# Splitting the overflow rows' sums on POOL into two half-precision parts for the scatter on TensorE

## The reference

```python
# layer 0
mask = (adj > 0.0)
h = relu(h[:, :, None, :] @ W1a + (h[:, :, None, :] - h[:, None, :, :]) @ W1b + b1)   # per edge j, k
hm = einsum('bjkh,bjk->bjh', h, mask)        # sum over the neighbours k of node j
x = x + hm @ W2 + deg[..., None] * b2
# layer 1
x = x + (adj @ relu(layernorm(x))) @ W3.T
```

## Time and profile before

| | us |
|---|---|
| median of 3 runs | 905.98 (905.89 to 906.07) |
| profiled execution | 904.65 |
| its span, first to last instruction | 902.6 |
| granted TensorE clock, mean | 0.983 |

### The profile page before, as it was taken

How to read it: one execution, slowest core, us unless ns; L and a number is a source line. 1 busy time by engine, 2 the same in 40 slices (tenths; PEclk the granted TensorE clock), 3 DMA queues, 4 the chain that set the end, 5 groups by cost and what they waited for, 6 DMA issues and landing times.

```text
span 902.6 us, 27715 instructions
## 1 busy us (share of the span) xinstructions
PE 862.0 (96%) x8626; PEld 771.7 (86%) x8627; DVE 866.4 (96%) x3032; ACT 775.9 (86%) x1728; POOL 698.8 (77%) x1548
## 2 busy tenths in 40 slices
PE   3879999999999999999999999999999999999996
PEld 1448999989998989999999999998999899989995
DVE  6989999999999999999999999999999999999993
ACT  4858989898989898989889898988898889898983
POOL 0857787888888888888887878787878788888874
PEclk9789999999999999999999999999999999999997
DMA  9700000000000000000000000000000000000000
GB/s 341 279 1 5 20 11 20 16 20 17 19 17 20 11 20 17 20 17 20 15 14 16 20 17 19 17 18 18 12 20 16 20 16 20 16 20 11 7 8 16
DMA packets 26549, 27.58 MB, mean 31 GB/s; under 512 B 3360, under 2 KB 24352, under 8 KB 25376
## 3 DMA queue, kind: packets, MB, share of 16 engines
q1 hardware_dynamic: 25488, 25.37, 8.3%
q10 hardware_dynamic: 912, 0.39, 0.2%
HBM read 21.56 MB, written 4.19 MB: 29 GB/s over the span
## 4 chain that ended last, share of the span: by engine, by line
PE 69%; DVE 19%; issue 5%; ACT 3%; POOL 2%; DMA 1%; SPq 0%; ACTq 0%; POOLq 0%; DVEq 0%
PE ring L378 36%; DVE acc L763 12%; PE ring L406 6%; PE post L465 4%; PE post L464 4%; PE prep L435 4%; PE post L470 4%; PE prep L445 3%; PE prep L442 2%; DVE onehot_space L749 2%; PE prep L441 2%; ACT ring L530 1%; POOL rstd L915 1%; DMA x_all<-x_nbf_dram 1%; DVE onehot_row L804 1%
## 5 line engine op out<-in xcount | busy, mean ns | idle before, releaser
L763 DVE SCALAR_TENSOR_TENSOR acc<-ring,acc 128x384 f32<-128x384 f32 x896 | 489.0, 546 | 1.1 <-PE ring L378 0.2
L530 ACT COPY ring<-P 128x768 f32<-128x768 f32 x512 | 403.3, 811 | 16.3 <-DVE acc L763 6.9
L378 PE MATMUL ring<-PQ,onehot_space 128*128 128x192 f16 x4096 | 404.0, 247 | 7.2 <-ACT ring L530 3.3
L378 PEld LDWEIGHTS ring<-PQ,onehot_space 128*128 128x128 f16 x4096 | 338.2, 100 | 31.7 <-ACT ring L530 19.2
L864 POOL TENSOR_TENSOR relu_row<-relu_row 128x192 f32<-128x192 f32 x256 | 151.8, 593 | 101.1 <-ACT relu_row L562 91.1
L749 DVE TENSOR_SCALAR onehot_space<-mask_all 128x512 f16<-128x512 f16 x512 | 155.2, 305 | 0.0
L583 ACT ACTIVATE h<-x_all,shift,rstd 128x64 f32<-128x64 f32 x128 | 56.3, 440 | 83.6 <-POOL shift L883 83.6
L851 POOL TENSOR_SCALAR start<-P,spare 128x192 f32<-128x192 f32 x128 | 121.1, 946 | 5.9 <-ACT P L576 5.1
L464 PE MATMUL post<-consts,acc 128*128 128x128 f32 x512 | 98.5, 274 | 1.5 <-POOL relu_row L864 1.5
L465 PE MATMUL post<-ownerT,relu_row 128*128 128x128 f32 x512 | 99.0, 275 | 0.0
L406 PE MATMUL ring<-PQ,owner 128*128 128x384 f16 (+1 forms) x512 | 94.1, 306 | 0.0
(11 more groups left out here) (129 smaller groups left out, 1616.0 us busy)
## 6 DMA issues: line engine op xcount, KB each, us to landing
onehot_space<-adj_kbj_dram SPq DMA_DIRECT2D x8, 1024.0 KB, 17.1
adj_again<-adj_kbj_dram SPq DMA_DIRECT2D x128, 64.0 KB, 1.9
x_all<-x_nbf_dram SPq DMA_DIRECT2D x8, 512.0 KB, 17.8
out_dram<-x_all SPq DMA_DIRECT2D x32, 128.0 KB, 1.7
consts<-consts_dram SPq DMA_DIRECT2D x1, 192.0 KB, 2.6
scratch<-w1a_dram ACTq DMA_DIRECT2D x2, 48.0 KB, 4.3
scratch<-w1b_dram ACTq DMA_DIRECT2D x2, 48.0 KB, 6.7
scratch<-b_dram ACTq DMA_DIRECT2D x1, 96.0 KB, 10.0
```

Of the source, the lines that this page charges most:

```text
L378: last = nc.tensor.matmul(to, hot(s), parts[:, part, H:2 * H], start=False, stop=(part == 1), skip_group_check=True)
L530: return nc.scalar.copy(slots[to], src.unsqueeze(1).unsqueeze(1).broadcast_to([N, BANKS, PER_BANK, H]))
L763: return nc.vector.scalar_tensor_tensor(sums, slots[to][:, bank_], 0.0, start[:, :, :] if first else sums, ALU.max, ALU.subtract if first ...
```

## The change

The overflow sums are no longer handed over in fp32. POOL adds the first two slots as before, adds the third and writes the result rounded to half precision (`high`), subtracts that from the sum of the first two, and adds the third slot to the difference, written in half precision (`low`). The four operations are chained by semaphores. The new tensor `hm_row` holds both parts, its last columns cleared once. Before writing it POOL also waits for a count of `transposed` that covers the matmuls of the graph before. `ownerT` becomes half precision. TensorE scatters the two parts with two half-precision matmuls in place of one fp32 matmul for each half of the hidden columns.

```diff
--- before.py
+++ after.py
@@ -139,12 +139,13 @@
         onehot_row = sb("onehot_row", [N, SLOTS, N], F16)
         from_first = sb("from_first", [N, N], F16)
         owner = sb("owner", [N, 2, N], F16)
-        ownerT = sb("ownerT", [N, 2, N])
+        ownerT = sb("ownerT", [N, 2, N], F16)
         code_row = sb("code_row", [N, N], F16)
         start = sb("start", [N, PER_BANK, H])
         acc_space = sb("acc", [N, 2, ROW + N - H2])
         acc = acc_space[:, :, 0:ROW].rearrange("p g (s h) -> p g s h", h=H)
         relu_row = sb("relu_row", [N, ROW_SLOTS, H])
+        hm_row = sb("hm_row", [N, 2, 2 * N], F16)
 
         sums_T = sb("sums_T", [N, 3, N])
         hmT, aggT = sums_T[:, 0:2, :], sums_T[:, 2, :]
@@ -227,6 +228,8 @@
         loop_half_summed = sem("loop_half_summed")
         loop_summed = sem("loop_summed")
         half_row_ready = sem("half_row_ready")
+        hm_high_ready = sem("hm_high_ready")
+        hm_rest_ready = sem("hm_rest_ready")
         hm_row_ready = sem("hm_row_ready")
         sums_T_ready = sem("sums_T_ready")
         bias_ready = sem("bias_ready")
@@ -457,12 +460,13 @@
                                 pe.wait_ge(loop_summed, load(nc.tensor, 0, b - 1) + load(nc.tensor, 1, b - 1) + 1)
                             pe.wait_ge(summed, b * REGULAR)
                             pe.wait_ge(hm_row_ready, b)
-                            hm_row = relu_row[:, :, :].rearrange("p s h -> p (s h)")
                             for k in range(2):
                                 for s in range(PER_BANK):
                                     hm = acc_space[:, (u + 1) % 2, s * H + k * N:s * H + (k + 1) * N]
                                     nc.tensor.matmul(sums_T_ps[:, k, :], hm, ident, start=(s == 0), stop=False, is_transpose=True)
-                                last = nc.tensor.matmul(sums_T_ps[:, k, :], hm_row[:, k * N:(k + 1) * N], ownerT[:, (u + 1) % 2, :], start=False, stop=True)
+                                for part in range(2):
+                                    last = nc.tensor.matmul(sums_T_ps[:, k, :], hm_row[:, part, k * N:(k + 1) * N], ownerT[:, (u + 1) % 2, :],
+                                                            start=False, stop=(part == 1))
                         if exists(b - 3):
                             pe.wait_ge(h2_ready, b - 2)
                             at, times = mixed_at(b, u, t)
@@ -635,6 +639,7 @@
             nc.vector.memset(w2b[H2:N, :], 0.0)
             nc.vector.memset(w3t[F:N, :], 0.0)
             nc.vector.memset(acc_space[:, :, ROW:], 0.0)
+            nc.vector.memset(hm_row[:, :, H:], 0.0)
             nc.vector.memset(start[:, :, :], 0.0).then_inc(loop_summed, 1)
             dve.wait_ge(consts_in, 16)
             nc.vector.tensor_tensor(upto, before, ident, ALU.add)
@@ -859,13 +864,17 @@
                 if exists(b - 1):
 
                     pool.wait_ge(relu_row_ready, b)
-                    sums = relu_row[:, 0, :]
-                    for s in range(1, ROW_SLOTS):
-                        last = nc.gpsimd.tensor_tensor(sums, sums, relu_row[:, s, :], ALU.add)
-                        if s < ROW_SLOTS - 1:
-                            last.then_inc(half_row_ready, 1)
-                            pool.wait_ge(half_row_ready, (b - 1) * (ROW_SLOTS - 2) + s)
-                    last.then_inc(hm_row_ready, 1)
+                    half, rest, third = (relu_row[:, s, :] for s in range(ROW_SLOTS))
+                    high, low = hm_row[:, 0, 0:H], hm_row[:, 1, 0:H]
+                    nc.gpsimd.tensor_tensor(half, half, rest, ALU.add).then_inc(half_row_ready, 1)
+                    if exists(b - 2):
+                        pool.wait_ge(transposed, b + 2)
+                    pool.wait_ge(half_row_ready, b)
+                    nc.gpsimd.tensor_tensor(high, half, third, ALU.add).then_inc(hm_high_ready, 1)
+                    wait_apart(pool, hm_high_ready, b)
+                    nc.gpsimd.tensor_tensor(rest, half, high, ALU.subtract).then_inc(hm_rest_ready, 1)
+                    wait_apart(pool, hm_rest_ready, b)
+                    nc.gpsimd.tensor_tensor(low, rest, third, ALU.add).then_inc(hm_row_ready, 1)
                 if exists(b - 3):
 
                     k = (u + 1) % 2
```

## The result

The changed kernel takes 1050.62 us (median of 4 runs, 1050.46 to 1051.89) against 905.98 us before. One of the four runs of the kernel before was a slow one, 2185.14 us, and is left out of its median. The ratio is 1.160 (95% interval 1.1577 to 1.1622). The forecast was 1052. The profiled execution took 1050.59 us, its span is 1048.6 us.

The account below looks back on a forecast made before the run. The prediction took the POOL-ScalarE loop (6.38 us per graph) as the bound. 121 periods growing from 6.48 to 7.63 us give 139 us, the ends 6.7 and 0.3: +146 on 904.65, plus 1.3: 1052 us, range 1022 to 1084.

Parts of the forecast that it names:

- The path: POOL's added work ahead of the second norm lengthens the POOL-ScalarE loop in full, +1.33 us per graph.
- the bound I had set: Each new POOL operation was bounded by two rows of the same width, 551 and 593 ns.
- The hop with two waits: Between POOL's first two adds, a second, long fulfilled wait adds 0 to 0.07 us, taken as 0.035.
- L880's operation: Power in POOL's second norm, 0.73 us mid-run and 0.57 at the end; half the difference taken, -0.08 us.
- 0.09 of slack: In ScalarE's part of the loop, a seed's wait for VectorE's last sum: 6.47 - 0.09 = 6.38 us.
- TensorE's saving: Half-precision scatter matmuls on TensorE save 0.2 us per graph, worth nothing while the loop binds.
- VectorE's own work: VectorE's work per graph without waiting in the kernel before, put at 6.3 us or more.
- the three bounds: Per graph in the kernel before: the loop 6.38 us, VectorE about 6.3, TensorE 6.14.
- faster: Rival, 3%: the fp32 scatter on TensorE bounds and POOL's additions vanish in its idle time, 884 us.
- POOL's order alone: Rival, 7%: ScalarE's wait for the shift does not close the loop; period 7.14 us, time 990 us.
- Longer operations beside VectorE: Rival, 6%: VectorE's work lengthens POOL's new operations, +0.48 us per graph, period 8.1 us, time 1110 us.
- TensorE's clock: Rival, 2%: TensorE's clock falls to half, 11.8 us per graph, about 1580 us.

Follow-up runs that it names:

- e5: Kernel before with one more POOL add of 192 fp32 columns per graph, last in POOL's step, outside the loop: 907.8 us, ratio 1.0005.
- e6: Kernel before with one more POOL add per graph between the overflow sums and the second norm, inside the loop: 954.9 us.
- e3: Changed kernel with ScalarE's h2 taking the first norm's scale and shift, so not waiting for POOL's second norm: 974.9 us.
- e1: Kernel before with POOL's four chained operations, the fp32 scatter on TensorE kept and the two extra results unused: 1042.6 us.
- e2: Changed kernel without POOL's subtract and last add, low part zero, TensorE's four half-precision matmuls kept: 915.3 us, ratio 1.0087.
- e4: Kernel before with ScalarE's h2 no longer waiting for POOL's second norm: 904.7 us, ratio 0.9972.
- e11: Kernel of e7 with two fp32 POOL adds per graph, started by VectorE's first sum, ahead of POOL's wait for the aggregate: 929.3 us, ratio 1.0240.
- e8: Changed kernel with POOL's second norm moved ahead of its overflow sums: 1274.4 us.
- e7: Kernel before without POOL's overflow sums; ScalarE writes three half-precision slots, TensorE scatters all three in half precision: 871.7 us, ratio 0.9607.
- e9: Kernel of e7 with one fp32 POOL add per graph, right after POOL's wait for VectorE's aggregate: 872.8 us, ratio 0.9633.
- e10: Changed kernel with POOL's wait on transposed moved from between the first two adds to ahead of the first: 1053.3 us.

## Why the prediction was right, and where it was not

**The path.** The forecast rested on one step: the added POOL work lies at the head of a loop that POOL and ScalarE close once per graph, so it adds in full. e5 against e6 shows the place, e3 shows the edge (76 us for one wait), e1 shows that POOL's part alone makes the loss. Right.

**The terms.** The chain is 509.58 - 506.92 = 2.66 us after, 1.27 before: +1.39 for a forecast of +1.33. I had taken 572 ns for each new operation; the second, third and fourth measured 593, 552 and 617. The third is the only one with a half-precision input and equals L890, so it is the input that makes POOL's operation shorter and not the output; the fourth lies 24 ns above the bound I had set. In e1 and e3 the same form took 593 and 591 ns, so the excess belongs to its place in time; in the changed kernel it starts at 508.96 while VectorE's owner operation runs (508.79 to 509.13). The inputs matter in another way that no run explains: the extra add of e5, fp32 with the same tile as both inputs, took 505 ns. The hop with two waits took the full 0.15 us, for 0.12 taken. L880's operation took 0.64 us, for 0.65 taken. The guess behind that term is borne out by the trace of the kernel before: where L880 meets VectorE's owner operation one of the two is long. In 102 graphs it is L880 (0.73 us, owner 0.34, as in the earlier trace rows), in 21 it is owner, as here:

```profile
94.30 0.36 DVE L798 SCALAR_TENSOR_TENSOR owner<-count_h,end_row,from_first 128x128 f16<-128x128 f16 x1
94.34 0.57 POOL L880 TENSOR_TENSOR rstd<-ve,half_power 128x1 f32<-128x1 f32 x1
```

ScalarE's part lost 0.13 us where I had counted 0.09 of slack: its seed starts 0.36 us after L560, not 0.41. Plus 0.06 and minus 0.05: the period came out within 0.01 us by errors that cancel, and so close a hit is luck.

**TensorE's saving.** I costed it at nothing, since L470 waits for h2 anyway. e1 and the waits (L474 stands 1.08 to 1.25 us) bear it out. The reasoning had more room than there was: the prediction gives L464 and L465 2.1 us from hm_row's being ready at 456.49, but TensorE, busy with its gathers, starts L464 only at 457.71. What L470 waited in the kernel before is 0.38 - 0.22 = 0.16 us; it is the change itself that makes the wait long. e2 adds that the saving was worth nothing before either.

**What bound the kernel before.** Here a step failed, though the time does not show it. I read VectorE's own work as about 6.3 us, from a gap of 0.29 us behind a bn_stats of 0.21, and took the loop at 6.38 for the longest of the three bounds. e4 shows VectorE at 6.5 with the loop cut: part of the 0.29 us was waiting, but other operations then take longer (from_first 565 ns instead of 437), so the wait was no slack. The loop was not the bound either. With ScalarE's unwaited part of 3.32 us in place of 3.45 it is 6.34 us long, 0.13 behind the period, which is about how long ScalarE's seed waited for VectorE's last sum (0.50 against 0.36 us after the eviction). That VectorE, and not TensorE, set the pace of the kernel before is argued and not shown: there TensorE is busy 596.80 of 600 us and VectorE 593.03, and what speaks for VectorE is that e2 takes work from TensorE without a gain and that VectorE is full in e2 and e4. The forecast survived because it started from the loop's own time and not from the period. The rival "faster" was priced at 884 us on the wrong 6.3; e2, with TensorE's part alone, has 915.

**The rivals.** POOL's order alone: 975 us when made real (e3), and not what happened. Longer operations beside VectorE: the means of POOL's new operations stayed within 25 ns of their bounds, but the meeting is real, and here VectorE pays: its one-hots went from a mean of 305 to 361 ns (from_first fell from 437 to 296), which VectorE's new slack of over 1 us hides. Three of them in the changed kernel, the second under POOL's L873 (507.66 to 508.25), the third under L856 (511.11 to 512.06), which has one tensor as input:

```profile
506.51 0.28 DVE L754 TENSOR_SCALAR onehot_space<-mask_all 128x512 f16<-128x512 f16 x1
...
507.95 0.45 DVE L754 TENSOR_SCALAR onehot_space<-mask_all 128x512 f16<-128x512 f16 x1
...
511.22 0.45 DVE L754 TENSOR_SCALAR onehot_space<-mask_all 128x512 f16<-128x512 f16 x1
```

The Trainium skill (GPSIMD Engine Reference, section 8 Key points) states the contention for VectorE instructions in a 2-port mode or with two SBUF inputs. The trace agrees that there is contention (0.28 to 0.45 us) and does not show in which mode an operation runs; e11 adds that either engine can be the one held up.

TensorE's clock: it stayed at 1.00, with TensorE 84% busy in 400 to 500 us. e8 makes the 2% for this rival look low: with waits of 1.7 to 2.1 in place of 1.2 us the clock falls in part of the graphs.

## What to carry to other kernels

When two engines wait for each other once per step, follow the loop through both in-order queues and add up its parts: work added inside it costs its full length, less what the loop has of slack (here 0.13 us), even on an engine with a fifth of its time idle, and the same work outside it costs nothing (907.8 against 954.9 us for one add). Before taking a busy engine for the bound, or the loop, cut one edge and see whether the period moves. And look at what an addition on POOL runs beside: a half-precision operation of VectorE can take more than twice as long there (0.55 for 0.22 us), or POOL's operation is the longer one, so work taken from POOL can be VectorE's gain (871.7 us in e7). A mean can hide this: look at single graphs.

## What the runs showed of the hardware that I had not expected

- POOL's add of 192 columns takes 593 ns with two fp32 inputs, whether it writes fp32 or half precision (L869, L873), and 552 with one half-precision input (L875). With one fp32 tile as both inputs it took 505 ns (e5, e9).
- Where an operation of POOL meets a half-precision one of VectorE, one of the two can be held up: in e11 from_first takes 0.55 us beside an add of 0.50, or 0.22 beside an add of 0.60, in about half of the graphs each; a one-hot goes from 0.28 to 0.45 us under POOL's L873 or L856.
- A second wait, fulfilled long before, costs POOL 0.07 us, in front of a late wait or behind the first operation (e10, the changed kernel).
- TensorE's granted clock fell to 0.50 again and again in e8, where TensorE waited 1.7 to 2.1 us for POOL in each graph, and stayed at 1.00 in the changed kernel, where it waited about 1.2 us of 7.6.
